# A graph layer on one core: index copy one tile sooner, waits by message group, results written straight to the output

## The reference

```
h = (xn @ W.T).reshape(n, H, D)                       # 8 heads of 32
alpha = <h[src], a_src> + <h[dst], a_dst> + sum(relu(edge_attr @ edge_W.T) * h[dst])
alpha = where(alpha >= 0, alpha, 0.2 * alpha)
ex = exp(alpha - segment_max(alpha, dst)[dst])
attn = ex / segment_sum(ex, dst)[dst]
gnn = segment_sum(h[src] * attn, dst)                 # 106250 edges
mix = (v + q2 @ (k2.T @ v) / sqrt(N)) @ W_out + b_out
x2 = x + gnn + mix
x3 = layernorm(x2)
ffn = sum over the top 2 of 8 experts: weight * (gelu((norm(x3) * lng_e + lnb_e) @ W1_e + b1_e) @ W2_e + b2_e)
out = x2 + ffn
```

## Time and profile before

| | us |
|---|---|
| three runs | 2914.71, 2921.71, 2924.52 (median 2921.71) |
| profiled execution, its own time | 2918.94 |
| its span | 2917.2 |
| edge stage, by the windows | about 238 to 1840 |
| routing | about 1864 to 2090 |
| experts | about 2095 to 2892 |
| last copy | 2894.7 to the end |

### The profile page before, as it was taken

The page is one execution under the profiler, slowest core; times in us unless marked ns, Lnnn a source line. Parts: engine busy times, 40 slices in busy tenths (PEclk is TensorE's granted clock), DMA queues, the critical chain, the costliest instruction groups (busy, mean ns, idle before and its releaser), DMA issues. The chain is left out here.

```text
span 2917.2 us, 34290 instructions
## 1 busy us (share of the span) xinstructions
PE 2098.4 (72%) x8607; PEld 1598.0 (55%) x8608; DVE 1494.7 (51%) x3105; ACT 582.7 (20%) x1504; POOL 1265.9 (43%) x1251
## 2 busy tenths in 40 slices
PE   5894777676666666666655654665399999999995
PEld 3572554454444444444433433554388888888885
DVE  7764676675667766666665656566312211221221
ACT  3551111111111111111101000333222222222221
POOL 5164555555656655566655543044322122222121
PEclk8896777877778877777887766876599999999998
DMA  8573443333333433333333332355232233222224
GB/s 261 191 262 109 117 113 109 108 111 106 111 107 110 115 99 104 109 107 110 107 92 101 100 85 63 114 187 163 96 66 59 40 63 64 37 36 64 64 37 109
DMA packets 184373, 306.88 MB, mean 105 GB/s; under 512 B 31898, under 2 KB 142852, under 8 KB 183492
## 3 DMA queue, kind: packets, MB, share of 16 engines
q0 software_dynamic: 71312, 179.36, 24.1%
q1 hardware_dynamic: 97580, 100.12, 11.2%
q10 hardware_dynamic: 15368, 26.22, 2.7%
HBM read 224.21 MB, written 87.78 MB: 107 GB/s over the span
## 5 line engine op out<-in xcount | busy, mean ns | idle before, releaser
L851 POOL DMA_INDIRECT hbuf<-table,recb x847 | 806.9, 953 | 332.3 <-issue 269.2
L938 PE MATMUL psum<-msg,ident 128*128 128x256 f32 x1840 | 606.6, 484 | 224.1 <-issue 165.7
L938 PEld LDWEIGHTS psum<-msg,ident 128*128 128x128 f32 x1840 | 445.8, 249 | 373.7 <-issue 200.8
L1125 DVE SCALAR_TENSOR_TENSOR prod<-psum,hd 128x1024 f32<-128x1024 f32 x230 | 280.6, 1220 | 517.5 <-DMA erow<-in_erow 471.2
L1577 POOL DMA_INDIRECT acc<-yo,id_now x104 | 161.5, 1553 | 639.8 <-DVE yo L1850 600.7
L1640 PE MATMUL psum<-f_xT,fw 128*128 128x256 f32 x1664 | 380.4, 387 | 32.6 <-issue 18.7
L1640 PEld LDWEIGHTS psum<-f_xT,fw 128*128 128x128 f32 x1664 | 322.4, 195 | 83.4 <-issue 21.8
L1650 PE MATMUL psum<-fw,hT 128*128 128x256 f32 x1664 | 367.8, 379 | 0.0
L1650 PEld LDWEIGHTS psum<-fw,hT 128*128 128x128 f32 x1664 | 312.1, 190 | 40.3
L1691 ACT ACTIVATE hT<-psum,fb 128x256 f32<-128x256 f32 x416 | 195.4, 474 | 600.7 <-PE psum L1640 540.3
L1128 DVE TENSOR_REDUCE al<-prod 128x32 f32<-128x1024 f32 x230 | 280.6, 1220 | 7.9
(11 more groups left out here) (324 smaller groups left out, 2361.2 us busy)
## 6 DMA issues: line engine op xcount, KB each, us to landing
xr<-xs SPq DMA_DIRECT2D x53, 260.0 KB, 2.7
hbuf<-table,recb POOLq DMA_INDIRECT x847
fw<-in_w ACTq DMA_DIRECT2D x12, 1024.0 KB, 7.2
table<-tab SPq DMA_DIRECT2D x49, 136.0 KB
hd<-hperm ACTq DMA_DIRECT2D x49, 136.0 KB
recs<-rec ACTq DMA_DIRECT2D x3, 2216.0 KB
xnd<-xn SPq DMA_DIRECT2D x49, 128.0 KB
xtd<-xT SPq DMA_DIRECT2D x49, 128.0 KB
```

Of the source, the lines that this page charges most:

```text
L851: pool.indirect_dma_start(hbuf[:, b, s, :], None, table, bass.IndirectOffsetOnAxis(ap=rec_i[:, b, s, REC // 2 - 1:REC // 2], axis=0)).then ...
L938: mm = pe.matmul(AC[:, 0:C], ident[:], msg[:, k % MR, s, :], start=(k == 0 and s == 0), stop=False, skip_group_check=True)
L1125: v.scalar_tensor_tensor(out=prod[:, k % 2, :, :], in0=Z[k % 2], scalar=0.0, in1=bc(hd[:, b, 0:C], 1, GS), op0=ALU.max, op1=ALU.mult).then ...
```

## The change

Three things, independent of one another:

1. ACT's `stage` for tile t+3 now stands behind `turned(t+2)` and ahead of `squares(t)`; it waits for the records of tile t+1, whose index buffer it takes. The prologue stages tile 2.
2. GpSimd loads two of its counts at the tile's head, and each of the third, fourth and fifth groups waits for its own count of tile t-2's messages: the third group's gathers for three, the fourth's for four, the fifth's for all (`old`), later groups for none more.
3. `acc` is gone. x2 rows go to `out` (the last tile 106 rows), the expert rows are added to `out`, with indices past the last row dropped. The last copy and its wait are gone.

```diff
@@ gpsimd, tile @@
                             older = None if isinstance(t, int) and t < 2 else groups_before(pool, t - 2)
+                            old = None if older is None else groups_before(pool, t - 1)
+                            rows = None if is_at(t, 0) or is_last(t) else rows_upto(pool, t - 1)
...
                                 if not is_at(t, 0):
-                                    gate(pool, ld_h[1 - b], rows_upto(pool, t - 1), passed)
+                                    gate(pool, ld_h[1 - b], rows, passed)
...
-                            if older is not None:
-                                gate(pool, msg_ready, groups_before(pool, t - 1), passed)
 
                             def further(k):
                                 with pool.If(n > k):
+                                    if older is not None and k <= 4:
+                                        gate(pool, msg_ready, old if k == 4 else older + k + 1, passed)
                                     for s in range(GS * k, GS * k + GS):
                                         gather(b, s)
@@ scalar, tile @@
-                            if not (is_last(t) or is_at(t, NT - 2)):
-                                after(act, ld_rec[b], 8 * (t - b) + 16)
-                                stage(t + 2, b)
                             after(act, al_ready, t + 1)
...
                                 turned(t + 2, b)
+                            if not (is_last(t) or is_at(t, NT - 2) or is_at(t, NT - 3)):
+                                after(act, ld_rec[1 - b], 8 * (t + b) + 16)
+                                stage(t + 3, 1 - b)
                             squares(t)
...
+                        after(act, ld_rec[0], 16)
+                        stage(2, 0)
@@ expert stage, sync @@
-                        sp.dma_start(acc[t * P:t * P + P, :], xm[:, t, :]).then_inc(st_x2, 16)
+                        full = min(P, N - t * P)
+                        sp.dma_start(out[t * P:t * P + full, :], xm[0:full, t, :]).then_inc(st_x2, 16)
...
-                    sp.dma_start(out.rearrange("(a b) c -> a (b c)", a=125),
-                                 acc[0:N, :].rearrange("(a b) c -> a (b c)", a=125)).then_inc(st_out, 16)
-                    sp.wait_ge(st_out, 16)
@@ expert stage, gpsimd @@
-                            pool.indirect_dma_start(acc, bass.IndirectOffsetOnAxis(ap=id_now[:, r:r + 1], axis=0),
-                                                    yo[:, r, :], None, compute_op=ALU.add).then_inc(st_y, 16)
+                            pool.indirect_dma_start(out, bass.IndirectOffsetOnAxis(ap=id_now[:, r:r + 1], axis=0),
+                                                    yo[:, r, :], None, bounds_check=N - 1, oob_is_err=False,
+                                                    compute_op=ALU.add).then_inc(st_y, 16)
```

More of the change, by code:

```diff
@@ L157, in gps_kernel @@
     xs = nc.dram_tensor("xs", [X * XCAP * FT, XW], F32).ap()
-    acc = nc.dram_tensor("acc", [NP + 2 * P, C], F32).ap()
     with ExitStack() as top:
@@ L1473, in gps_kernel @@
                     "tmpl_ready", "info_ready", "st_tail", "st_x2"))
-            (ld_b, ld_xr, x_mm, xt_ready, h_mm, gelu_done, y_mm, y_out, st_y, w_used, y_rows, f_dve, st_out, x_read, y_sent) = (
+            (ld_b, ld_xr, x_mm, xt_ready, h_mm, gelu_done, y_mm, y_out, st_y, w_used, y_rows, f_dve, x_read, y_sent) = (
                 sem("f_" + s, rf) for s in ("ld_b", "ld_xr", "x_mm", "xt_ready", "h_mm", "gelu_done", "y_mm", "y_out",
-                                            "st_y", "w_used", "y_rows", "dve", "st_out", "x_read", "y_sent"))
+                                            "st_y", "w_used", "y_rows", "dve", "x_read", "y_sent"))
             ld_q = [sem(f"ld_q{i}", rf) for i in range(QR)]
```

## The result

| | kernel before | changed kernel |
|---|---|---|
| five runs each, median | 2918.99 us (2910.13 to 2924.52) | 2943.66 us (2931.51 to 2952.72) |
| ratio to before, 95% interval | | 1.0084 [1.0052, 1.0115] |
| profiled execution, span | 2917.2 | 2929.8 |
| mean granted clock of TensorE | 0.826 | 0.807 |

Slower by 24.7 us at the medians; 2943 was forecast. The profiled execution of the changed kernel, 2931.51 us, is the quickest of its five, so the two traces differ by 12.6 us only.

What follows compares the result with a forecast made beforehand. TensorE's results were taken to come late while GpSimd streams gathers, all at once some 3 us after it pauses. 2918.94 - 22.1 (end) + 46 (edge stage) = 2943 us; range 2840 to 3010, the forecast's own 2930 to 2980.

Steps and rivals of the forecast that it cites:

- the end: Last microseconds: with the copy out<-acc gone, the span ends where the last pair of adds has landed, -22.1 us.
- the edge stage: Edge-stage term: GpSimd's stop is moved, not removed; +1.0 us a tile over 46 tiles, +46 us (worked sum +91).
- the prediction's own signs of being wrong: Edge stage: gathers wait for messages under 4 us a tile, or the score starts while GpSimd streams; then the stage is shorter.
- What is late next: Five-group tile: GpSimd's stop moves from the fetch to the fourth group's gathers, 7.54 us, 7.24 over the usual gap.
- if TensorE is let go 3.07 us after the stop as now: Edge stage: TensorE's held result, and so the score, comes 3.07 us after GpSimd's new stop begins.
- The head: Head of the next tile: first gathers wait for two messages of the tile before, a new wait of 1.5 us.
- I price the move at nothing: Two count loads moved to the tile's head cost nothing, GpSimd's sequencer running ahead; uncovered, bounded by one 2.98 us a tile.
- the 2998 of the forecast's sum with that floor: Total if two uncovered count loads per tile at about 600 ns each added an estimated +55 us; 2998 us.
- The four-group price: Edge stage, 16 four-group tiles: longer stop, scatter's wait and head wait make +4.1 us a tile, +66 us.
- the pair in the earlier trace: Two edge-stage tiles, one fetch without a wait: 62.7 us against 64.3, -0.8 us a tile, -35 over 46 tiles.
- Slower by far: Rival: no early release, every tile pays the worked price or more; 2988 up to 3073 us, middle 3010; chance 0.14.
- The edge stage faster: Rival: fetch stops are truly spare once per-group waits replace them; 2862 us, in the limit 2712; chance 0.25.

Runs made afterwards that it cites:

- Runs 1 and 5: 1: kernel before with only the last copy removed, 2478.23 us, ratio 0.9941; 5: changed kernel, unchanged, where the kernel before took 2496, 2468.78 us, ratio 0.9893.
- Run 9: Changed kernel plus a GpSimd pause of three waited-for memsets behind each record fetch: 2835.79 us, one run, where the kernel before took 2920.78.
- Run 7: Kernel before with the index copy one tile sooner and results straight to the output, old message wait kept: 2956.53 us, ratio 1.0115.
- run 8: Changed kernel with gathers of 544 bytes instead of 1088: 2971.73 us, where the kernel before took 2921.

## Why the prediction was right, and where it was not

**The sum.** 2943 forecast, 2943.7 measured. That it is this close is luck: two terms were off and made up for each other almost wholly, the end by +6.4 us (-22.1 forecast, -15.7) and the edge stage by about -6 (+46 forecast, +40 by the medians, +29 by the two traces), and within the edge stage the prices by kinds of tile were off by more. Both of the prediction's own signs of being wrong there came out: the gathers wait for messages 40.7 us in all, 0.8 us a tile and not over 4, and the third score starts while GpSimd streams. The stage was not shorter for that, because the stop had gone to a place that the prediction did not price at its full size.

**The end: mis-sized.** The step "With it gone the span ends where the last pair of adds has landed" failed. It left out what lay beside the copy: 6.4 us of closing on GpSimd's queue, in both traces. Runs 1 and 5 have it too, 6.43 us each.

**What bounds the kernel: right, at this level.** TensorE's results come late while GpSimd streams and mostly arrive some 3 us after it stops (3.07 in the forecast; 3.1 at the median of the signals in both kernels, from 1.1 to 4.7), and the stop at the fetch was not pure loss. Run 9, one run, shows it from the other side: adding stops gains 108 us. Run 7 shows that taking this one stop away costs 51.

**What is late next: wrong place.** I had GpSimd stop 7.5 us at the fourth group's gathers for a message. It stops at the scatter, for the tile's sum, 4 to 10 us, and the gathers wait for messages only 40.7 us in all. The step that failed is "if TensorE is let go 3.07 us after the stop as now": the third score's result was not held at all (TensorE's encoding from 990.22 to 990.81, the score at 990.85), since GpSimd had gone on only at 985.13, after its two stops; the held ones were the last score's and the closing product of the tile (42 of 46).

**The head: right that it waits, for another reason.** 1.5 us for messages was forecast; it is 3 to 4 us in the tiles shown, and the loads of counts are its largest part. "I price the move at nothing" failed: its condition, that the sequencer runs ahead, ended with the wait at the scatter. The 2.98 us that I kept as its bound is close to the 3.17 it costs, but by chance: in the stop of the earlier trace rows the loads had been done under gathers by 982.87, and what stood in the stop was a wait and a branch of GpSimd's queue that took 0.70 us each. The Trainium skill ("DMA: Bandwidth & Descriptors", Latency and other measured facts) gives such a load a floor of about 600 ns. The trace agrees for the whole step, 0.54 to 0.63 us from one load to the next, of which the load itself is 0.28. The stop also lets results through, so its price is not simply added: the 2998 of the forecast's sum with that floor would have been 54 us too high.

**By kinds of tile.** Five groups +37.8 (forecast +31), six -22.0 (forecast -6), four +14.0 (forecast +66). The four-group price was the wrong one: they too have two stops, and what the stops let through may have given most of it back, which was not tried; the three-group tiles, priced at nothing, lost 13.4. Taking +1.0 a tile instead of the worked +2.0 because of the pair in the earlier trace rows was what made the sum right. It was a choice between two worked values, and no run shows that pair's gain as such.

**The rivals.** "Slower by far" did not come. "The edge stage faster" is what happens where results are not held: the condition I named, that TensorE's results come while GpSimd still streams, holds at the 2494 level, and there the change gains 1.1%. That this can differ from one job to the next was in none of my cases.

**Still open.** What holds the results. Their release follows GpSimd's stops; the gathers' bytes do not decide it (run 8); the gathers are not slowed (953 and 956 ns for the kernel before at the two levels); and it was present or absent for a whole job. No run tells why; whether another chip or what else ran on the machine decides it wasn't tried. The kernel that would be best at both levels wasn't found: 2836 against 2919 with pauses at one, 2469 against 2496 with the change alone at the other.

One rival is untested: the recording of the traces itself. The five traces of the slower level (both kernels, runs 7 to 9) differ from the nine of the faster one in two more ways. Vector gives 753 signals on semaphores of its own between the first and the last softmax; the nine have 752 or 753 of them, the five only 440 to 500, so records are missing. And in the same stretch of the five, 14 to 216 of the instructions of GpSimd's queue other than loads and waits took 0.65 to 0.75 us, where the longest of them in the nine took 0.17. Both would fit a recorder that falls behind and holds up the engines that write to it, and neither proves it. Every execution here has a recorded span and clock, so no time on record tells whether the 2919 level exists without recording.

## What to carry to other kernels

A wait that looks needless may be what lets other engines' results through: before it is taken away, look at what starts within a few microseconds of the moment it begins, and ask which wait takes its place. What a removed last transfer gives is the distance from its start to the end less what was hidden beside it, such as the closing work of another queue. And when the same kernel has two levels of time 17% apart, a change must be measured at both: this one is a gain at one and a loss at the other. Before such a level is taken for the kernel's own, count the records in the trace: here the level with the late results is also the one with missing records.

## What the runs showed of the hardware that I had not expected

- A pause of 4 us in GpSimd's stream of indirect DMAs, once a tile, made the kernel 108 us faster at one level (2943.7 to 2835.8, one run) and 172 us slower at the other (2468.8 to 2640.9).
- At the slower level TensorE's closing product of 967.14 was signalled at 979.63 and seen by vector at 979.66; at the faster, ACT started 0.04 us after the product it waited for. Two later signals of TensorE came within 0.15 us of it. TensorE's mean granted clock is lower there: 0.803 to 0.831, against 0.859 to 0.871 at the faster level in the runs without long pauses (0.842 to 0.846 with them).
- At the slower level, instructions of GpSimd's queue that took at most 0.17 us at the faster one took 0.70 us in places (197 of 1158 in the kernel before), and signals are missing from the trace.
- GpSimd's queue takes 6.43 us to close at the end of the program, beside other work (2894.8, kernel before) or alone (2923.1, changed kernel); run 8 had 6.60.
